# GpSimd pauses in the middle of a group's gathers until the first half has landed (graph network, two convolution layers)

## What is computed

```python
def _gcn_conv(x, edge_index, edge_weight, W, b):
    row, col = edge_index + self-loops
    deg = segment_sum(ew, col);  dis = rsqrt(deg)
    norm = dis[row] * ew * dis[col]
    h = x @ W.T
    return segment_sum(h[row] * norm[:, None], col) + b

x = x + relu(_gcn_conv(layer_norm(x), ..., W6, b6))
x = x + relu(_gcn_conv(layer_norm(x), ..., W7, b7))
return x @ Wp.T + bp
```

## Time and profile before

| | |
|---|---|
| median of 3 executions | 6131.06 us (6126.41 to 6134.06) |
| the profiled execution | 6161.81 us, its span 6160.0 us |
| mean granted TensorE clock | 0.761 of 2.4 GHz |
| busy: TensorE, its weight loads, VectorE, ScalarE, GpSimd | 63%, 46%, 44%, 12%, 52% |
| gathers in all, their queue's share of the 16 DMA engines | 3328, 27.7% |
| layer one, first gather to the last | 66.0 to 1344.8 us |
| layer two, first gather to the last | 1415.7 to 2752.0 us |

### The profile page before, as it was taken

How to read it: one execution, slowest core, us unless ns; L and a number is a source line. 1 busy time by engine, 2 the same in 40 slices (tenths; PEclk the granted TensorE clock), 3 DMA queues, 4 the chain that set the end, 5 groups by cost and what they waited for, 6 DMA issues and landing times. The chain is left out here.

```text
span 6160.0 us, 73788 instructions
## 1 busy us (share of the span) xinstructions
PE 3909.5 (63%) x14574; PEld 2847.9 (46%) x14575; DVE 2717.3 (44%) x9904; ACT 718.7 (12%) x2361; POOL 3225.9 (52%) x3351
## 2 busy tenths in 40 slices
PE   3555555563665566654676766666674777777777
PEld 2343434342444344443555555555552555555555
DVE  5443434343233323332444444444453555555555
ACT  3000000000000000000111111101010222121222
POOL 5466666645555555655444444444423555555553
PEclk8677777776777777776777777777776888888889
DMA  7344444433333333333333333333322344444442
GB/s 182 80 107 106 107 106 107 106 87 90 108 108 107 105 106 107 108 99 90 89 91 100 91 98 91 98 94 96 96 75 85 109 122 115 119 119 114 121 114 84
DMA packets 334355, 636.43 MB, mean 103 GB/s; under 512 B 86166, under 2 KB 213124, under 8 KB 333828
## 3 DMA queue, kind: packets, MB, share of 16 engines
q0 software_dynamic: 159744, 441.43, 27.7%
q1 hardware_dynamic: 170437, 185.56, 9.7%
q10 hardware_dynamic: 3648, 3.67, 0.2%
HBM read 565.59 MB, written 64.79 MB: 102 GB/s over the span
## 5 line engine op out<-in xcount | busy, mean ns | idle before, releaser
L1192 POOL DMA_INDIRECT g_G<-t,srcI x832 | 810.2, 974 | 925.1 <-DVE g_Gp L1390 686.1
L1785 POOL DMA_INDIRECT g_G<-t,srcI x832 | 791.5, 951 | 626.3 <-PE g_ps L2152 365.5
L227 POOL DMA_INDIRECT g_G<-t,srcI x832 | 818.5, 984 | 518.8 <-issue 238.5
L849 POOL DMA_INDIRECT g_G<-t,srcI x832 | 796.4, 957 | 541.2 <-ACTq L1114 302.3
L2142 PE MATMUL g_psA<-g_win,g_ohT 128*128 128x257 f32 x1664 | 613.9, 456 | 369.6 <-issue 187.0
L727 PE MATMUL g_ps<-g_G,g_oh 128*128 128x257 f32 x1664 | 550.3, 496 | 141.7 <-DVE g_oh L577 139.3
L1519 PE MATMUL g_psA<-g_win,g_ohT 128*128 128x4 f32 x1664 | 345.1, 328 | 439.0 <-issue 429.1
L1887 DVE CUSTOM_DVE_ANT_0 g_junk<-g_G,g_psA 128x257 f32<-128x257 f32 x832 | 348.0, 418 | 569.2 <-DMA g_G<-t,srcI 245.8
L1519 PEld LDWEIGHTS g_psA<-g_win,g_ohT 128*128 128x128 f32 x1664 | 360.1, 317 | 459.5 <-issue 459.2
L2152 PE MATMUL g_ps<-g_G,g_oh 128*128 128x257 f32 x1664 | 560.1, 423 | 2.3 <-issue 2.3
L2142 PEld LDWEIGHTS g_psA<-g_win,g_ohT 128*128 128x128 f32 x1664 | 319.1, 216 | 503.0 <-issue 232.1
(11 more groups left out here) (373 smaller groups left out, 5050.1 us busy)
## 6 DMA issues: line engine op xcount, KB each, us to landing
g_G<-t,srcI POOLq DMA_INDIRECT x3328
g_relb<-relrow SPq DMA_DIRECT2D x104, 512.0 KB
t<-g_t SPq DMA_DIRECT2D x53, 132.0 KB
g_rec<-t SPq DMA_DIRECT2D x53, 132.0 KB
g_own<-t SPq DMA_DIRECT2D x53, 129.5 KB
x<-g_o SPq DMA_DIRECT2D x53, 128.5 KB
g_rec<-x SPq DMA_DIRECT2D x53, 128.5 KB
t<-g_t4r SPq DMA_DIRECT2D x53, 128.5 KB
```

The source lines that it names most:

```text
L227: pool.indirect_dma_start(G[:, b, u, 0:width], None, m.t1, IOA(ap=m.srcI[:, g * UW + u:g * UW + u + 1], axis=0)).then_inc(s_g[b][u // QW], 16)
L849: pool.indirect_dma_start(G[:, b, u, :], None, table, IOA(ap=m.srcI[:, g * UW + u:g * UW + u + 1], axis=0)).then_inc(s_g[b][u // QW], 16)
L1192: pool.indirect_dma_start(G[:, b, u, :], None, m.t3, IOA(ap=m.srcI[:, g * UW + u:g * UW + u + 1], axis=0)).then_inc(s_g[b], 16)
L1785: pool.indirect_dma_start(G[:, b, u, :], None, m.t4, IOA(ap=m.srcI[:, g * UW + u:g * UW + u + 1], axis=0)).then_inc(s_g[b][u // QW], 16)
```

## The change

In layers one and two GpSimd waits, from the fifth group on, before it issues the ninth gather of the group (u == 2 * QW). It waits for the semaphore of the second quarter of this group's own buffer to reach the count that it has when the gathers u = 4 to 7 of this group have landed. Layers three and four are as before.

```diff
@@ first_layer, gpsimd
                 for u in range(UW):
+                    if g >= NBW and u == 2 * QW:
+                        pool.wait_ge(s_g[b][1], (g // NBW + 1) * 16 * QW)
                     pool.indirect_dma_start(G[:, b, u, 0:width], None, m.t1,
                                             IOA(ap=m.srcI[:, g * UW + u:g * UW + u + 1], axis=0)).then_inc(s_g[b][u // QW], 16)
```

## The result

The changed kernel takes 6164.74 us (median of 7 runs, 6146.16 to 6181.68), the kernel before beside it 6128.12 us (7 runs, 6114.9 to 6134.06): ratio 1.0062, 95% interval 1.0044 to 1.0079, some 37 us slower where I had forecast 97 us faster. The profiled execution took 6164.7 us (span 6162.9), that of before 6161.8; the one of before lies above all seven timed runs, so the two traces differ by 3 us where the medians differ by 37, and what follows goes by the two changed layers.

The account below looks back on a forecast made before the run. The prediction took hand-overs between engines, delayed by runs of gathers, to bound the kernel. Layer one -14 and layer two -83 us, others 0, sum to -97: 6131 - 97 = 6034 us, range 5940 to 6195.

Parts of the forecast that it names:

- What bounds the kernel: Layers one and two: runs of gathers delay hand-overs between engines; a gather is worked off in about 1.43 us, issued in 1.25.
- The size of the wait: Before the ninth gather in layers one and two: 2.92 us after the eighth, so later gathers start 1.67 us later.
- That idle time pays for it: Layers one and two: GpSimd's chain of 21.7 us stays below steps of 23.7 and 25.9, so the wait costs nothing.
- So the run of sixteen becomes two runs of eight with an empty queue between: Layers one and two: eight gathers are worked off by 11.4 us, before the ninth starts at 11.7.
- Rival (a): Layers one and two: halves of neighbouring groups join into runs of sixteen, +38 and +24 us, 6193 us; chance 0.26.
- Rival (b): Layers one and two: delay hangs on all sixteen gathers however spaced, still ending at 23.2 us; 6131 us; chance 0.12.
- Layer one forecast -14: Layer one: step falls from 23.7 to 23.4 us, -0.3 us x 48 = -14 us.
- Layer two forecast -83: Layer two: step falls from 25.94 to 24.2 us, -1.74 us x 48 = -83 us.
- a floor of the working off: Shortest step in layers one and two: 16 x 1.43 = 22.9 us plus 0.5 to GpSimd's next start, 23.4 us.
- Layers three and four at 0: Layers three and four: no change in time, because they do not hold the added wait.
- Rival (c): Layers one and two: working off is no limit, GpSimd becomes the bound at 21.7 us a step; 5833 us; chance 0.06.
- The argument from ports: Whole kernel: by the skill's port rule gathers could not slow groups and time would stay; the prediction decided against drawing that.

Follow-up runs that it names:

- the sections run: Kernel before, with stretches of groups plain, paused mid-group, paused twice, paced by 256-column memsets, or paused four times, all layers: 5851.84 us against 6134.36, ratio 0.9542.
- the second profile: Profile from timing the whole change once more, unaltered, against the kernel before: 6116.85 us against 6078.22, ratio 1.0061.

## Why the prediction was wrong

- **What bounds the kernel: right as far as tested.** Hand-overs are late in runs of gathers, a run ends as if one gather were worked off in 1.43 to 1.45 us, and spacing the gathers, each layer in its own way, takes 11% off. What does the working off no run shows.
- **The size of the wait: right.** Forecast 2.92 us from the eighth gather to the ninth, measured 3.10 and 3.01 us in the mean; GpSimd's chain 20.8 and 20.7 us to the start of the sixteenth gather. That idle time pays for it held on the holding machine (layer one steps 23.6 us with the pause and without); where GpSimd is the bound, it costs 1.75 to 1.98 us a group.
- **"So the run of sixteen becomes two runs of eight with an empty queue between": this step failed.** The prediction took the 3.84 and 5.5 us of idle time between groups as given. They were there because the group was late. Once a group ends in 17 to 18 us, GpSimd does not stop, and halves of two groups join. Nor does the pause empty a run of sixteen: it needs 16 x 1.44 = 23.0 us, and the next half begins 601.02 - 578.71 = 22.3 us after its start. So the next eight hang on it as well, which makes 24.
- **Rival (a) is what happened**, with steps of 22.1 and 25.0 us in layer one. Its inside was different: it had the next group's small steps held until 34.6 us and 14 us of work behind them, while in layer one the small steps came on time (0.13 to 0.19 us in the mean) and the last hand-over, ScalarE's move, was held for 24 gathers and not 16. Its +38 us for layer one was too much (-4), its +24 for layer two too little (+33): its sum of +62 stands against +29 in the traces of the two layers and +37 in the medians. What I held against it ("it needs the very gain to come first, and a late group puts the pause back") is no objection: it came first, and the pause came back in every second group, which is the alternation.
- **Rival (b) is out**: it had the hold end at 23.2 us as before, while in a clear group of layer one ScalarE follows TensorE by 0.14 us.
- **The terms.** Layer one forecast -14, measured -4. Layer two forecast -83, measured +33. With the halves kept apart ten of its groups take 24.3 us, forecast 24.2, but that is luck: the forecast added 0.8 us to a floor of the working off, and what was measured is GpSimd's pass with two pauses. Layers three and four at 0: the traces have them 14 and 4 us shorter, with no change in them, but layer three held the largest gain of all.
- **Rival (c), GpSimd as the bound, was priced as a gain.** On a prompt machine it is the truth, and there a pause is pure loss. On the holding machine it comes true only with spaced gathers or two pauses, at 23.2 to 24.4 us and not at 21.7.
- **The argument from ports.** The prediction drew from the Trainium skill, SBUF — State Buffer, section "SBUF: two separate sides", that gathers could not slow the group. That section of the Trainium skill speaks of ports, which cannot contend, and not of hand-overs. On the holding machine ScalarE's move came 4.0 to 7.4 us after TensorE's end in all 47 steps of layer one of the kernel before, on prompt machines 0.13 us; no run here shows a wait for a port.

## What to carry to other kernels

Before you count on an idle time, ask what made it: a speed-up may remove the very gap on which it stands, and then look for steps that alternate between two values. Spacing a stream of gathers by a little in every place (0.14 us here) can do more than one large pause, and costs less. Such a gain belongs to the conditions in which it was measured: time the kernel on more than one machine, and more than once, before keeping it.

## What the runs showed of the hardware that I had not expected

- The same kernel takes 6078 to 6134 us on some machines and 4476 to 4481 us on others. On both, a gather is issued every 1.25 us. What differs is the hand-over in a run of gathers: ScalarE's move in layer one comes 5.6 us after TensorE's end in the mean on the one kind, 0.13 us on the other. The mean granted clock of the kernel before differs too, 0.75 to 0.77 and 0.87 to 0.88. Since the hold begins after TensorE's end, I do not take the clock for its cause, but no run tests it. What makes the difference stays open.
- Signals from TensorE are the ones held (the delays here include what an engine still does before it in its own order). In the plain stretches of the sections run ScalarE's move starts 5.4 us after TensorE's end in layer one and 4.2 in layer two, where VectorE also takes the product after 4.4 us and ScalarE its three transposes after 7.0 in sum; on a prompt machine, with the change's pause in layer two, these last three are 0.13, 0.15 and 1.1. The statistics that VectorE hands to ScalarE, and the root that goes back, come within 0.15 us in the same groups.
- The end of a hold counts the gathers of the run: 1.45 us each for 16, 1.44 for 24 in 22 of 23 pairs of layer one (1.43 in the second profile), 1.42 for 64.
